# Two stages of a gated transformer kernel in one block: the last stage's first steps in the third's last rounds, and its final reads issued together

## The reference, cut to what matters

```python
x = x + tanh(g_xattn[0]) * xattn0(layernorm(x), ctx)   # 16-head cross attention
x = x + tanh(g_ffn[0])   * soft_moe(layernorm(x))      # 16 experts of 16 slots
x = x + tanh(g_xattn[1]) * decoder(layernorm(x), ctx)  # causal self-, cross-attention, 1024-wide MLP, three layer norms
x = x + tanh(g_ffn[1])   * moe(layernorm(x))           # 8 experts, each token's two best, plus a shared gated MLP
```

## Time and profile before

| what | value |
|---|---|
| three runs | 1106.19, 1109.22 (median), 1110.18 us |
| profiled execution, its own time | 1107.69 us |
| its span in the profile | 1105.9 us |
| busy over the span: PE, DVE, ACT, POOL | 88%, 72%, 51%, 33% |
| third stage, turns 16 to 18 | about 712 to 747 us |
| last stage, first `up` matmul | 770.38 us |
| last expert tile copied out, first row read issued | 1050.9, 1054.6 us |

### The profile page before, as it was taken

How to read it: one execution, slowest core, us unless ns; L and a number is a source line. 1 busy time by engine, 2 the same in 40 slices (tenths; PEclk the granted TensorE clock), 3 DMA queues, 4 the chain that set the end, 5 groups by cost and what they waited for, 6 DMA issues and landing times. The chain is left out here.

```text
span 1105.9 us, 22667 instructions
## 1 busy us (share of the span) xinstructions
PE 971.9 (88%) x6445; PEld 826.0 (75%) x6445; DVE 791.4 (72%) x2253; ACT 566.3 (51%) x1333; POOL 361.6 (33%) x551
## 2 busy tenths in 40 slices
PE   4899999999996768999999999963778889999973
PEld 3677677676764446999999999863667779999962
DVE  3677777777762425888888888865666748888767
ACT  1578777787774613344344443314545255656520
POOL 1111212112110003445344453432676604444410
PEclk9999999999998958999999999995989989999996
DMA  7776857768800310101001010201324224444367
GB/s 163 155 143 134 157 103 160 135 134 152 172 4 1 110 45 29 47 26 49 25 25 49 25 49 25 73 1 48 110 98 130 92 58 122 125 127 129 94 215 242
DMA packets 85873, 104.40 MB, mean 94 GB/s; under 512 B 15070, under 2 KB 75438, under 8 KB 85808
## 3 DMA queue, kind: packets, MB, share of 16 engines
q1 hardware_dynamic: 77616, 81.91, 31.8%
q0 software_dynamic: 7632, 21.05, 5.3%
q10 hardware_dynamic: 560, 0.66, 0.2%
HBM read 38.50 MB, written 57.62 MB: 87 GB/s over the span
## 5 line engine op out<-in xcount | busy, mean ns | idle before, releaser
L1607 POOL DMA_INDIRECT expert_out<-early_weights,aim x71 | 69.8, 984 | 101.9 <-DVE aim L1936 82.0
L1145 ACT ACTIVATE f_hidden<-c_hidden,f_b 128x256 f32<-128x256 f32 x128 | 53.7, 470 | 68.3 <-PE c_hidden L1334 68.3
L1598 POOL DMA_INDIRECT sorted_rows<-m_z,slot_i x64 | 72.1, 1127 | 42.8 <-DVE slot_i L1816 24.9
L1332 PE MATMUL c_mlp<-f_w_hi,f_hidden_hi 128*128 128x256 f32 x256 | 80.7, 315 | 3.6 <-DVE f_hidden_lo L1263 3.6
L1332 PE MATMUL c_hidden<-y2T_hi,f_w_hi 128*128 128x256 f32 x256 | 77.1, 301 | 0.0
L595 DVE TENSOR_REDUCE mx<-ps_scores 128x8 f32<-128x616 f32 x64 | 50.8, 794 | 36.3 <-PE ps_scores L681 36.3
L747 PE MATMUL ps_probT<-ident,prob 128*77 128x128 f32 x512 | 69.7, 280 | 3.4 <-DVE probT L358 1.7
L1334 PE MATMUL c_mlp<-f_w_hi,f_hidden_lo 128*128 128x256 f32 x256 | 72.4, 283 | 0.0
L1333 PE MATMUL c_mlp<-f_w_lo,f_hidden_hi 128*128 128x256 f32 x256 | 72.4, 283 | 0.0
L1334 PE MATMUL c_hidden<-y2T_hi,f_w_lo 128*128 128x256 f32 x256 | 72.3, 282 | 0.0
L1333 PE MATMUL c_hidden<-y2T_lo,f_w_hi 128*128 128x256 f32 x256 | 72.2, 282 | 0.0
(11 more groups left out here) (335 smaller groups left out, 3145.4 us busy)
## 6 DMA issues: line engine op xcount, KB each, us to landing
sorted_rows<-no_row SPq DMA_DIRECT2D x15, 2322.0 KB, 14.4
m_z<-sorted_rows SPq DMA_DIRECT2D x71, 129.0 KB, 2.1
early_weights<-expert_chunks SPq DMA_DIRECT2D x8, 640.0 KB, 4.4
combT<-combineT_all SPq DMA_DIRECT2D x16, 256.0 KB, 2.3
slT<-slots_all SPq DMA_DIRECT2D x16, 256.0 KB, 2.5
early_weights<-expert_out SPq DMA_DIRECT2D x8, 512.0 KB, 6.4
early_weights<-expert_out POOLq DMA_DIRECT2D x8, 512.0 KB, 6.3
out<-x_all SPq DMA_DIRECT2D x8, 512.0 KB, 3.5
```

The lines of the kernel that those rows point to most:

```text
L1145: last = act.activation(hf[:, q % 2, j, :], psH[:, q % 2, j, :], ACT.Relu, bias=fb1[:, c_:c_ + 1])
L1332: pe.matmul(out, lh, rh, start=start, stop=False, skip_group_check=shared)
L1598: pool.indirect_dma_start(out=sorted_rows[:, :], in_=zn[:, s % 3, t, :], in_offset=None, out_offset=bass.IndirectOffsetOnAxis(ap=slot_i[:, ...
L1607: pool.indirect_dma_start(out=expert_out[:, :], in_=xo[:, i % 3, :], in_offset=None, out_offset=bass.IndirectOffsetOnAxis(ap=aim_i[:, i % ...
```

## The change

The third stage's and the last stage's engine programs are put one behind the other in one block; the block end, `clear_signals` and the second block start are gone (`phase_c` returns its programs and keeps its semaphores). The last stage's buffers lie on memory that is dead by then: the first of them on the combine weights and slots (free when the last `mix` is done), the expert weights `eh` and `el` behind them, so that `expert_hi(0)` waits for the last `mlp_out` and the last `x3`. The last stage's programs on POOL, ACT and DVE become generators with `yield` between steps, and the third stage's list gets five places `("ahead", k)` in its `LAST` group at which the next piece is executed, in turns 16 to 18 only. The chunk loads on SP move from behind the third stage's loop to ahead of it. `stats(0)` and `stats(1)` are executed ahead of the constants. At the end all eight blocks' expert rows are read at once, into `eh` and `el`, whose weights are dead by then; the output writes follow all of SP's reads; `combine` stands ahead of `hidden` in each unit, and `combine(6)` ahead of `result(7)`. The PSUM buffers of the last stage are allocated in another order.

```diff
+def ahead(program, places):
+    def step(b, k):
+        if isinstance(b, int) and (b, k) in places:
+            next(program)
+    return step
...
-                        self.phase_c(c)
-            self.clear_signals()
+                        third = self.phase_c(c, whole)
             with ExitStack() as c:
-                self.phase_d(c)
+                self.phase_d(c, third)
...
+        order = [(LAST, "ahead", 0), (SELF, "slot_outputs"), (MLP, "mlp_in", 0), (SELF, "so_out"),
...
+                 (CROSS, "ca_scores"), (SELF, "x2"), (MLP, "hidden_hi", 0), (LAST, "mean_c"), (LAST, "rstd_c"),
+                 (LAST, "ahead", 1), (MLP, "hidden_lo", 0), (CROSS, "ca_max"), (CROSS, "ca_bias"),
...
+                 (MLP, "y2_bias"), (LAST, "ahead", 2), (MLP, "hidden_out", 2), (SELF, "y0"), (MLP, "hidden_lo", 1),
...
+                 (MLP, "hidden_out", 3), (SELF, "sa_scores"), (LAST, "ahead", 3), (MLP, "mlp_out", 2),
...
+                 (MLP, "mlp_out", 3), (SELF, "residual1"), (SELF, "stats_a"), (SELF, "mean_a"), (SELF, "rstd_a"),
+                 (LAST, "ahead", 4)]
...
             load_ctx(0)
             load(1)
+            for n in range(SC):
+                sp.dma_start(self.stage_shared(n), ins["shared_chunks"][:, n]).then_inc(chunk_in.sem, 16)
+            sp.dma_start(self.stage_expert(0), ins["expert_chunks"][:, 0]).then_inc(chunk_in.sem, 16)
             with sp.Fori(1, NB - 1) as b:
...
+                                  ahead=ahead(program, [(NB - 3, 2), (NB - 2, 1)])), NB)
...
+                                 ahead=ahead(program, [(NB - 3, 1), (NB - 3, 2), (NB - 3, 3), (NB - 2, 4)])), NB)
...
+                                 ahead=ahead(program, [(NB - 3, 1), (NB - 3, 3), (NB - 2, 0), (NB - 2, 1), (NB - 2, 2), (NB - 2, 3),
+                                                       (NB - 1, 1), (NB - 1, 3)])), NB)
...
-        back = early[:, 0:2 * 2 * BT * D].rearrange("p (s i n) -> p s i n", s=2, i=2)
+        spare = [w[:].rearrange("p e n -> p (e n)").bitcast(F32) for w in (eh, el)]
+        back = [spare[c // 4][:, c % 4 * 2 * BT * D:(c % 4 + 1) * 2 * BT * D].rearrange("p (i n) -> p i n", i=2) for c in range(NBLK)]
...
             for c_, b in enumerate(TURN):
-                if c_ >= 2:
-                    sp.wait_ge(sum_done.sem, 2 * (c_ - 2) + 1)
-                sp.dma_start(back[:, c_ % 2, 0], kept[:, 0, b]).then_inc(back_in[0][c_ % 2].sem, 16)
-                if c_ >= 1:
-                    sp.wait_ge(sum_done.sem, 2 * c_)
-                    sp.dma_start(Y[:, TURN[c_ - 1]], X[:, TURN[c_ - 1]]).then_inc(o_out.sem, 16)
-            sp.wait_ge(sum_done.sem, 2 * NBLK)
-            sp.dma_start(Y[:, TURN[-1]], X[:, TURN[-1]]).then_inc(o_out.sem, 16)
+                sp.dma_start(back[c_][:, 0], kept[:, 0, b]).then_inc(back_in[0][c_].sem, 16)
+            for c_, b in enumerate(TURN):
+                sp.wait_ge(sum_done.sem, 2 * (c_ + 1))
+                sp.dma_start(Y[:, b], X[:, b]).then_inc(o_out.sem, 16)
...
-                if c_ >= 2:
-                    pool.wait_ge(sum_done.sem, 2 * (c_ - 2) + 2)
-                pool.dma_start(back[:, c_ % 2, 1], kept[:, 1, b]).then_inc(back_in[1][c_ % 2].sem, 16)
+                pool.dma_start(back[c_][:, 1], kept[:, 1, b]).then_inc(back_in[1][c_].sem, 16)
...
+            act.wait_ge(third["mixed"].sem, NB)
+            act.wait_ge(third["chunks"].sem, 16 * (SC + 1))
+            for n in range(SC):
+                shared_hi(n)
+                yield
             act.wait_ge(made.sem, 2)
             rows_in(0)
+            yield
             rows_in(1)
-            for n in range(SC):
-                shared_hi(n)
             zf_out(0, 0)
             zf_out(0, 1)
             z_hi(0)
+            act.wait_ge(third["multiplied"].sem, 4 * NB)
+            act.wait_ge(third["finished"].sem, NB)
             expert_hi(0)
...
             for m in range(BESIDE, NBLK * SC):
+                combine(m - BESIDE)
                 hidden(m)
                 hidden_lo(m)
                 if m == BESIDE:
                     z_lo_turned(1)
-                combine(m - BESIDE)
+            combine(NBLK - 2)
             result(NBLK - 1)
-            combine(NBLK - 2)
             combine(NBLK - 1)
...
+        @block.vector
+        def _(dve):
+            program = vector_last(dve)
+            third["vector"](dve, program)
+            deque(program, 0)
```

More of the change, by code:

```diff
@@ L1 @@
+from collections import deque
 from contextlib import ExitStack
@@ L1077, in _, with scalar_third @@
             run(pool, order, dict(rstd3=lambda b: rstd("l3", b), shift3=shift3, rstd_a=lambda b: rstd("la", b), rstd_b=lambda b: rstd("lb", b),
-                                  rstd_c=lambda b: rstd("lc", b), y2_bias=y2_bias, hidden_hi=hidden_hi), NB)
-        @block.scalar
-        def _(act):
+                                  rstd_c=lambda b: rstd("lc", b), y2_bias=y2_bias, hidden_hi=hidden_hi,
+                                  ahead=ahead(program, [(NB - 3, 2), (NB - 2, 1)])), NB)
+        def scalar_third(act, program):
             act.wait_ge(bias_done.sem, 1)
@@ L1753, in _, with vector_last @@
                     z_turned(1, 1)
-        @block.vector
-        def _(dve):
+        def vector_last(dve):
             def shared_lo(n):
@@ L1886, in tile_table @@
                 dve.tensor_tensor(topd[:], top[:], spread(top[:, :, 0:1], 2, 8), ALU.subtract).then_inc(table.sem, 1)
+            for f in range(2):
+                stats(f)
+                yield
             dve.wait_ge(filled.sem, 2)
@@ L1896, in _ @@
             dve.tensor_scalar(base[:], experts[:], float(TOKENS), None, ALU.mult).then_inc(made.sem, 1)
-            dve.wait_ge(made.sem, 2)
-            for f in range(4):
-                stats(f)
+            yield
             for n in range(SC):
                 shared_lo(n)
+                yield
+            for f in (2, 3):
+                stats(f)
+                yield
+            dve.wait_ge(made.sem, 2)
             z_lo(0)
@@ L2189, in _ @@
             down(NBLK * SC - 1)
+        block = c.enter_context(nc.Block())
+        @block.sync
+        def _(sp):
+            third["sync"](sp)
+            sync_last(sp)
+        @block.gpsimd
+        def _(pool):
+            program = gpsimd_last(pool)
+            third["gpsimd"](pool, program)
+            deque(program, 0)
+        @block.scalar
+        def _(act):
+            program = scalar_last(act)
+            third["scalar"](act, program)
+            deque(program, 0)
+        @block.vector
+        def _(dve):
+            program = vector_last(dve)
+            third["vector"](dve, program)
+            deque(program, 0)
+        @block.tensor
+        def _(pe):
+            third["tensor"](pe)
+            tensor_last(pe)
 def spread(ap, dim, n):
```

79 lines of the change are left out of this document (34 added, 45 removed).

## The result

| | median | runs | ratio to the kernel before |
|---|---|---|---|
| before | 1109.70 us | 4, 1106.19 to 1110.23 | |
| changed | 1097.86 us | 4, 1094.46 to 1100.94 | 0.9899 [0.9858, 0.9940] |

The change makes the kernel 1.0% faster, about 11 us (11.8 between the medians). That is inside the predicted range (1097.0 to 1109.5), but near its end, and well over the predicted gain of 4.2 us. The profiled execution took 1100.06 us; its span is 1098.3 us, 7.6 less than before. Of that, 2.1 us are there already at the thirteenth `residual3` of the third stage (689.40 against 691.48), where both kernels have done the same work but for the weight loads on SP. So places are counted from there in what follows.

The account below looks back on a forecast made before the run. A serial start-up chain of 28.65 us bounded the boundary, VectorE the tail. Head 3.4 + tail 0.8 = 4.2 us off 1107.69 gives 1103.5, off the median 1105.0; stated 1104.3, range 1097 to 1109.5.

Parts of the forecast that it names:

- likeliest case: Whole kernel: the time range of the likeliest case alone, 1100.5 to 1107.7 us; forecast gain 1.5 to 7, chance 0.58.
- the gaps take it: Rival at the stage boundary: inserted steps fit into idle time, R hardly moves; gain 10.3 us, 1097.4; chance 0.22.
- R to the first `up`: Stage boundary: from the start of `residual3(15)`, called R, to the last stage's first `up`, 28.65 us falls to 19.1.
- slip of R: Third stage's last rounds: steps put ahead delay the start of `residual3(15)` by 3.4 + 2.7 = 6.1 us.
- head up to the first `up`: Stage boundary: first `up` at 766.9 instead of 770.38, a gain of 3.4 us after the slip.
- tail, read to end: Tail on VectorE: two read waits go, 2.3 us gained, a later start loses 1.5; net gain 0.8 us.
- The step that failed: Start-up chain: `rows_in(1)` on ScalarE follows `rstd(1)`, which needs `stats(3)`; 2.9 us to R + 10.3, then R + 12.4.
- The constants and `shared_lo` at zero: Turn 17 on VectorE: constants and three `shared_lo` cost zero, hidden by waits for GpSimd and TensorE; otherwise 3.6 us.
- The barrier at 0.97 us: Stage boundary: block end, clearing and block start, 748.00 - 747.03, are removed outright, 0.97 us.
- The chain only re-forms: Rival at the head: collisions and unforeseen waits of `rows_in(1)` eat its gain; 1107 to 1109 us; chance 0.12.
- The first pair comes late: Rival in the tail: first reads land only with all sixteen; tail loses 15.7 us, whole 1120; chance 0.08, or worse.

Follow-up runs that it names:

- tail_only: Kernel before with only the new tail (all reads at once, `combine` ahead of `hidden`), old stage boundary kept: ratio 0.9998 [0.9987, 1.0009].
- wait_rstd1: Changed kernel with one wait more, `rows_in(1)` on ScalarE waiting for `rstd(1)`: ratio 0.9988 [0.9968, 1.0008].
- rstd0_late: Changed kernel with `rstd(0)` on GpSimd at place 3 of turn 17 instead of place 1: ratio 0.9904 [0.9879, 0.9929].
- head_only: Changed kernel with the tail's old order (two reads in flight, output writes between, `combine` behind the unit): ratio 0.9902 [0.9882, 0.9921].
- best: Changed kernel with the edits of `old_order`, `rstd0_late` and `z_first` together: ratio to the kernel before 0.9862 [0.9832, 0.9893].
- block_only: Changed kernel, one block without barrier, but no last-stage step put ahead into the third stage: ratio 0.9937 [0.9913, 0.9961].
- old_order: Changed kernel with all sixteen reads still at once, but `combine` behind the unit as before: ratio 0.9902 [0.9878, 0.9926].
- z_first: Changed kernel with `z_lo(0)` ahead of `stats(2)` and `stats(3)` on VectorE: ratio 0.9899 [0.9865, 0.9932].
- pair_first: Changed kernel with the first pair of reads issued alone, the other fourteen once it has landed: ratio 0.9913 [0.9883, 0.9943].

## Why the prediction was right, and where it was off

The direction and the place were right: the head gains, the tail gives nothing that can be measured. The gain was 2.6 times what was predicted, and two large terms behind it were both wrong, with opposite signs: the chain 9.8 us too long, the slip 4.9 us too short. That the time still lies in the stated range is partly luck. It is below the likeliest case (1100.5 to 1107.7), and the range reached down to it only because it took in most of the rival "the gaps take it", whose mechanism did not happen.

| step of the prediction | predicted | measured |
|---|---|---|
| R to the first `up` | 28.65 to 19.1 | 28.65 to 9.33 |
| slip of R | 6.1 | 10.95 |
| head up to the first `up` | gain 3.4 | gain 8.4 |
| tail, read to end | gain 0.8 | loss 0.5 (`tail_only`: gain 0.1) |

- **The step that failed** is "`rstd(1)` on GpSimd needs `stats(3)` and takes 2.9: R + 10.3. `rows_in(1)` stands ahead of `zf_out(0, 0)`: R + 12.4." `rstd(0)` makes the factors of blocks 0 and 1, and `rows_in(1)` needs only it. `wait_rstd1` puts the dependency in and gets 19.09 us and 0.9988, so this one term is worth 9.8 us. The clock hangs on it too: with the shorter chain TensorE is granted 0.97 from R to the first `up`, and the sixteen `logits` matmuls take 2.05 us; in `wait_rstd1` it idles 12.7 us, and they take 3.79. The rows shown before could have told it: the second group of four activations starts at 759.50, while the last row of `rstd(1)` starts at 760.66. A row that starts before its supposed releaser ends has another releaser.
- **The slip was mis-sized**, 10.95 against 6.1 us. By where it comes in (each against the same step before, counted from the thirteenth `residual3`): 4.7 up to `y2T_lo`, the low half of the MLP's input for sequence 15, predicted 3.4, as `ca_bias` took 1.75 us beside `y2_bias`, against 0.17; 1.5 more at the first hidden quarter, where TensorE, having idled 2.5 us, was granted 0.80 in the window from 725.3 to 734; 3.4 for `rstd(0)`, predicted 2.7, its slowest step being 2.20 us beside `shared_lo(1)`, where it took 1.67 both times in the kernel before, at 754.97 beside `stats` and at 758.49 beside nothing; and 1.3 at the last quarters, clock 0.57 behind 3.15 idle us. `rstd0_late` confirms the last two, 4.0 us of the 4.7. The collision has a price as well: `head_only` runs the same program up to R, its `ca_bias` took 0.17 us, and from `y2_scale(15)` on everything is 1.3 us earlier, R at 59.90, although TensorE was granted 0.61 at 708 to 712, where the changed kernel had 1.00. `best` against `rstd0_late` gives 1.3 us too (55.91, 57.19). The 1.5 us of the hidden quarter rest on the rows alone. Two executions without any step ahead (`tail_only`, `block_only`) had R at 52.6 and 52.3, with a granted clock of 0.69 and 0.75 at 708 to 712 and 1.00 before, and `ca_bias` at 0.91 and 0.83 us. So some 2 us of such a slip also come without the change, and against these two it is 8.7 us.
- **The constants and `shared_lo` at zero** held: no wait of TensorE or ScalarE is put down to them; only the 0.5 us on `rstd(0)`'s slowest step are theirs. The Trainium skill (SBUF — State Buffer, "SBUF: two separate sides") had that collision in its rule, and the trace agrees with it, in kind and below the 1.3 us that the prediction allowed for it.
- **The barrier at 0.97 us** fits the rows (1.1 us by `block_only`'s `stats(0)`), and no run shows it alone. The 5.1 us of `block_only` between R and `up` are mostly the last stage's new order, which the prediction had in its chain.
- **The tail**, predicted +0.8, measured -0.5: the two waits went, as said, but POOL's first read came after 7.0 us and not 5.5, and these 1.5 us are about the difference. The prediction took a landing from rows with few reads in flight for a queue of sixteen. `old_order` shows what it had not seen: in the profile 3.6 us lay in the new place of `combine`, TensorE's clock behind its empty 3 us included.
- **The rivals.** "The gaps take it" had nearly the right time (1097.4) by the wrong means: R did move. "The chain only re-forms" is what `wait_rstd1` shows. "The first pair comes late" is there with 1.5 us, nowhere near its 15.7.
- **What stays open.** 2.3 us are given back between the first `up` and the first read, in a stretch that varies by 3 us between executions of equal code. The profiles show 7.6 us, the medians 11.8: the profiled execution of the changed kernel is 2.2 us slower than its median, that of the kernel before 2.0 faster. The changed kernel's runs alone spread over 6.5 us. Single edits that save 2 to 4 us in the profile (`rstd0_late`, `z_first`, `old_order`) leave the ratio at 0.990, so what each is worth in time is open. How much of the head's gain is the barrier and how much the new order is open too.

## What to carry to other kernels

Before a dependency goes into a sum, hold each of its rows against the start of what it is to release: a start ahead of the end rules it out. When steps are put early into a pipeline whose engines have no slack, put them behind the instruction that feeds the bottleneck engine, not ahead of it, since the engine that is made to wait can lose clock afterwards, as TensorE did here behind 2.5 and 3.15 idle us. When a run takes away a barrier and keeps a new order, don't book its gain on the barrier: follow the chain and see which of the two each microsecond belongs to. When transfers are issued at once, leave work that needs none of them in front of the first consumer.

## What the runs showed of the hardware

- A VectorE instruction on 128x2 numbers took 1.75 us instead of 0.17 where GpSimd's addition of 128x512 had started 0.90 us ahead of it (713.86). In two runs, `head_only` and `best`, VectorE's started 0.01 us ahead of GpSimd's and took 0.17. Then the next VectorE instruction, `y3_center`, took 1.91 us (0.93 in the changed kernel), and yet all that follows came 1.3 us earlier. The rows of `head_only`:

```profile
711.85 0.17 DVE L1244 TENSOR_SCALAR c_small_cbias<-c_small_cmax 128x2 f32<-128x2 f32 x1
711.86 1.30 POOL L1074 TENSOR_TENSOR y2b<-y,f_rows 128x512 f32<-128x512 f32 x1
711.93 1.91 DVE L1185 SCALAR_TENSOR_TENSOR xg_lc<-r,mv_lc,f_rows 128x256 f32<-128x256 f32 x2
```

- TensorE's granted clock fell in some executions and not in others behind the same idle time: behind 2.38 us it was 0.69 at 708 to 712 in `tail_only` and 1.00 at 712 to 716 in the kernel before.
- Sixteen queued reads of 512 KB moved 380 to 420 GB/s once under way. The first read of the first queue landed after 3.2 to 3.4 us in every run, the first of the second queue after 6.4 to 7.1, with four reads in flight after 5.5 and 6.0 (the kernel before, `head_only`), alone with its partner after 5.0. The Trainium skill (DMA: Bandwidth & Descriptors, "Queues, rings and completion order") has the engines take the queues in turns and each ring in order. The trace agrees for the order, in that the first pair lands before the later ones; its second read is late all the same.
- In the four profiles from the second chip ScalarE stood two or three times for 4 to 6.5 us between 820 and 880 us (in `pair_first` 5.96 us up to 833.98), and the profile names only "remote" or "issue"; the earlier ones have no such wait. It goes with the longer stretch from `up` to read in all four, and its cause is open.
